# Roots and halves through PSUM, heads in pairs, DMA transposes of q and k, and values one pair back

## What is computed

```python
x = _rmsnorm(tokens, norm_w)
q = x @ Wq
k, v = jnp.split(x @ Wkv, 2, axis=-1)          # 16 heads of 64
q = _head_rmsnorm(q, q_gamma); k = _head_rmsnorm(k, k_gamma)
sim = jnp.einsum('bhid,bhjd->bhij', q, k)
sim = jnp.tanh(sim / SOFTCLAMP) * SOFTCLAMP
attn = jax.nn.softmax(sim * DIM_HEAD ** (-0.5), axis=-1)
out = jnp.einsum('bhij,bhjd->bhid', attn, v)
return out.transpose(0, 2, 1, 3).reshape(b, n, HEADS * DIM_HEAD) @ Wo
```

## Time and profile before

| | before |
|---|---|
| median of 3 runs | 1263.25 us (1262.8 to 1263.63) |
| the profiled execution | 1261.8 us, its span 1259.8 us |
| busy, share of the span | PE 93%, ACT 86%, DVE 82%, POOL 73% |
| matmuls | 13897 |
| mean granted TensorE clock | 0.992 of full |

### The profile page before, as it was taken

The page is one execution under the profiler, slowest core; times in us unless marked ns, Lnnn a source line. Parts: engine busy times, 40 slices in busy tenths (PEclk is TensorE's granted clock), DMA queues, the critical chain, the costliest instruction groups (busy, mean ns, idle before and its releaser), DMA issues.

```text
span 1259.8 us, 36165 instructions
## 1 busy us (share of the span) xinstructions
PE 1165.6 (93%) x13897; PEld 972.3 (77%) x13897; DVE 1032.2 (82%) x2153; ACT 1082.2 (86%) x2055; POOL 917.6 (73%) x1105
## 2 busy tenths in 40 slices
PE   3789999999999999999999999999999999999988
PEld 2468887778877778878778878778878778878777
DVE  6788889888889888889888889888889888888862
ACT  3589898889898889888888988888988888988885
POOL 4477777777777777877777877777777777777663
PEclk9899999999999999999999999999999999999999
DMA  4000000000000000000000000000000000000000
GB/s 132 10 11 11 14 16 7 15 15 11 15 15 7 15 15 11 15 15 7 15 15 11 14 16 7 15 15 11 14 15 7 15 15 15 10 11 11 11 6 9
DMA packets 32224, 19.41 MB, mean 15 GB/s; under 512 B 3508, under 2 KB 31288, under 8 KB 32056
## 3 DMA queue, kind: packets, MB, share of 16 engines
q1 hardware_dynamic: 32056, 17.12, 4.7%
HBM read 12.13 MB, written 4.19 MB: 13 GB/s over the span
## 4 chain that ended last, share of the span: by engine, by line
PE 42%; DVE 25%; ACT 19%; issue 11%; POOL 1%; ACTq 0%; POOLq 0%
PE ps_scores L481 8%; ACT probs L563 6%; PE ps_aux L455 5%; DVE qk L729 4%; PE ps_aux L448 4%; PE ps_aux L406 4%; PE ps_y L525 4%; DVE heads_T L738 3%; DVE sel_rows L760 3%; DVE qk L694 3%; PE ps_aux L408 3%; PE ps_aux L407 3%; ACT L596 3%; DVE norm L667 3%; ACT hid L596 3%
## 5 line engine op out<-in xcount | busy, mean ns | idle before, releaser
L905 POOL TENSOR_TENSOR probs_lo<-probs 128x512 f16<-128x512 f32 x512 | 586.3, 1150 | 235.1 <-ACT probs L563 232.9
L555 ACT ACTIVATE clamped<-ps_scores 128x512 f32<-128x512 f32 x512 | 310.3, 606 | 124.5 <-PE ps_scores L481 124.4
L563 ACT ACTIVATE probs<-clamped 128x512 f32<-128x512 f32 x512 | 324.9, 635 | 0.4
L503 PE MATMUL ps_o<-v_hi,probs 128*128 128x65 bf16 x2048 | 240.0, 195 | 4.5 <-DVE o_sb L706 2.7
L504 PE MATMUL ps_o<-v_lo,probs 128*128 128x64 bf16 x2048 | 239.2, 193 | 0.0
L505 PE MATMUL ps_o<-v_hi,probs_lo 128*128 128x65 bf16 x2048 | 238.9, 194 | 0.0
L481 PE MATMUL ps_scores<-heads_T 64*128 64x256 f16 x3072 | 212.9, 271 | 14.2 <-ACT clamped L555 14.0
L406 PE MATMUL ps_aux<-w_hi,xhT_hi 128*128 128x512 f32 x384 | 191.5, 499 | 31.9 <-DVE qk L729 21.6
L503 PEld LDWEIGHTS ps_o<-v_hi,probs 128*128 128x128 bf16 x2048 | 192.1, 99 | 30.1 <-issue 18.2
L504 PEld LDWEIGHTS ps_o<-v_lo,probs 128*128 128x128 bf16 x2048 | 189.8, 99 | 5.0
L505 PEld LDWEIGHTS ps_o<-v_hi,probs_lo 128*128 128x128 f16 x2048 | 190.2, 98 | 0.0
(11 more groups left out here) (83 smaller groups left out, 2211.2 us busy)
## 6 DMA issues: line engine op xcount, KB each, us to landing
x_in<-in_L_attn_tokens_dram SPq DMA_DIRECT2D x32, 128.0 KB, 2.3
x_res<-in_L_attn_tokens_dram SPq DMA_DIRECT2D x32, 128.0 KB, 2.3
out_dram<-y_sb SPq DMA_DIRECT2D x32, 128.0 KB, 1.9
sel_raw<-xn SPq DMA_DIRECT2D x192, 4.0 KB
qk<-in_L_attn_Wkv_dram SPq DMA_DIRECT2D x2, 512.0 KB, 5.4
qk<-in_L_attn_Wq_dram SPq DMA_DIRECT2D x1, 512.0 KB, 3.6
qk<-in_L_ffn_W_dram SPq DMA_DIRECT2D x2, 256.0 KB
hid<-in_L_attn_q_gamma_dram SPq DMA_DIRECT2D x1, 512.0 KB, 7.0
```

Of the source, the lines that this page charges most:

```text
L503: pe.matmul(full, hi[:, col], v_hi[:, par, u, h], start=(u == 0), stop=False)
L555: nc.scalar.activation(clamped[:, buf], ps_scores[:, s % SCORE_BANKS], ACT.Tanh).then_inc(clamp_done, 1)
L563: nc.scalar.activation(probs[:, buf], clamped[:, buf], ACT.Exp, bias=LIFT, scale=SOFTCLAMP * DH ** -0.5).then_inc(probs_done, 1)
L905: g.tensor_tensor(probs_lo[:, buf], probs[:, buf], probs[:, buf].bitcast(BF16)[:, 1::2], ALU.subtract).then_inc(lo_made, 1)
```

## The change

Heads go in twos: a step has 8 slots, each with a pair. Tanh and exp take both banks of scores as one instruction of 1024 columns, `clamped` has one buffer and `probs` two pairs. The values of a pair come one slot later, at the end of the slot, and are divided in the slot after. `ps_o` is one bank in place of two. In the rest of that bank lie `rnorm`, `minus_half_norm2` and `newton_a`; the bank freed is `ps_n`. The roots start from the PSUM tile in two seeds and take nine instructions on VectorE; GpSimd no longer has a part in them. `normalise` does one pair at a time, from `qk` into `ps_n`, four pairs ahead of the scores; ScalarE rounds `ps_n` to f16 (`half`), VectorE subtracts (`halves`), and SyncE turns each half with a DMA transpose into `heads_T` (`turn_heads`); the matmul transposes `qkT` are gone. The selection and the normalisation of the input go from VectorE to GpSimd, and the turned inputs `xhT` and `xnT` share one task `xT`. Since TensorE must not write a bank that VectorE uses, `values` waits for the steps of its slot that touch `ps_o`.

```diff
+RING = 2
+VALUES_LAG = 1
+DIVIDE_LAG = 2
+
+SCALAR_STEPS = [
...
+    [("tanh",), ("half",), ("exp",), ("hid", 0, 0), ("hid", 1, 0)],
...
 VECTOR_STEPS = [
...
+    [("halves",), ("divide",), ("newton", 0), ("newton", 1), ("newton", 2), ("newton", 3), ("newton", 4),
+     ("newton", 5), ("normalise",)],
...
 POOL_STEPS = [
...
+    [("bias",), ("lo",)],
+    [("select",), ("lo",)],
...
-        ps_o = ctx.enter_context(nc.psum_tensor("ps_o", [P, 2, 512], F32))
+        ps_o = ctx.enter_context(nc.psum_tensor("ps_o", [P, 512], F32))
         ps_aux = ctx.enter_context(nc.psum_tensor("ps_aux", [P, AUX_BANKS, 512], F32))
+        ps_n = ctx.enter_context(nc.psum_tensor("ps_n", [P, 512], F32))
...
-                elif kind == "qkT":
-
-                    if k % 2 == 0:
-                        wait(pe, qk_normed, 4 * b + k // 2 + 1)
-                    for j in range(2):
-                        for t in range(TT):
-                            at = j * HEADS * DH + k * P
-                            ins = pe.transpose(bank[:, (j * TT + t) * P:(j * TT + t + 1) * P],
-                                               qk[:, par, t, at:at + P], ident[:])
...
             def scores(st, pair):
...
-                wait(pe, qkT_split, PAIRS * b + pair + 1)
-                wait(pe, clamp_done, HEADS * b + 2 * pair)
+                wait(pe, heads_turned[pair % 4], 32 * ((PAIRS * b + pair) // 4 + 1))
+                wait(pe, clamp_done, PAIRS * b + pair)
...
-            def values(st, ahead, h):
+            def values(st, s, ahead, pair):
 
                 b, par, _ = st.batch(ahead)
-                pair = h // 2
-                if h == 0:
+                if pair == 0:
                     wait(pe, v_split, 4 * b + 4)
-                wait(pe, lo_made, HEADS * b + h + 1)
-                if h % 2 == 0:
-                    wait(pe, o_normed, PAIRS * b + pair - 1)
-                buf = h % RING
-                hi = probs[:, buf].bitcast(BF16)[:, 1::2]
-                for t in range(TT):
-                    at = (t * 2 + h % 2) * (DH + 1)
-                    full = ps_o[:, pair % 2, at:at + DH + 1]
-                    for u in range(TT):
-                        col = slice(u * seq + t * P, u * seq + (t + 1) * P)
-                        pe.matmul(full, hi[:, col], v_hi[:, par, u, h], start=(u == 0), stop=False)
-                        pe.matmul(full[:, 0:DH], hi[:, col], v_lo[:, par, u, h], start=False, stop=False)
-                        ins = pe.matmul(full, probs_lo[:, buf, col], v_hi[:, par, u, h],
-                                        start=False, stop=(u == TT - 1))
+                wait(pe, lo_made, PAIRS * b + pair + 1)
+                wait(pe, o_normed, PAIRS * b + pair)
+                n = st.batch(0)[0]
+                wait(pe, qk_normed, min(PAIRS * n + s + NORMALISE_LEAD + 1, PAIRS * batches))
+                if s == 2:
+                    wait(pe, seed_made, min(2 * (n + 2), 2 * batches))
+                if s in (3, 4):
+                    wait(pe, newton_step, min(9 * (n + 2) - (3 if s == 3 else 0), 9 * batches))
...
+            def turn_heads(st, ahead, pair):
+
+                b, _, _ = st.batch(ahead)
+                wait(sp, scores_done, 2 * PAIRS * (b - 1) + 2 * pair + 2)
+                for half, made in enumerate((half_hi_made, half_lo_made)):
+                    sp.wait_ge(made, PAIRS * b + pair + 1)
+                    sp.dma_start(heads_T[:, half, pair].rearrange("p t j n -> p (t j) n"),
+                                 halves16[:, pair % 4, half].rearrange("p a n -> p (a n)"),
+                                 transpose=True).then_inc(heads_turned[pair % 4], 16)
...
+            def tanh(st, pair):
+                b, _, _ = st.batch(0)
+                wait(act, scores_done, 2 * PAIRS * b + 2 * pair + 2)
+                wait(act, probs_done, PAIRS * b + pair)
...
+            def half(st, ahead, pair):
+                b, _, _ = st.batch(ahead)
+                act.wait_ge(qk_normed, PAIRS * b + pair + 1)
+                wait(act, heads_turned[pair % 4], 32 * ((PAIRS * b + pair) // 4))
+                nc.scalar.copy(halves16[:, pair % 4, 0].rearrange("p a n -> p (a n)"), ps_n[:]).then_inc(half_hi_made, 1)
...
+                wait(dve, newton_step, 9 * b + k)
+                if k % 3 == 0:
+                    v.tensor_tensor(newton_a, newton_r[:], minus_half_norm2, ALU.mult).then_inc(newton_step, 1)
+                elif k % 3 == 1:
+                    v.tensor_tensor(newton_a, newton_a, newton_r[:], ALU.mult).then_inc(newton_step, 1)
+                else:
+                    if k == 8:
+                        wait(dve, qk_normed, PAIRS * b)
+                    v.scalar_tensor_tensor(rnorm if k == 8 else newton_r[:], newton_a, 1.5, newton_r[:],
+                                           ALU.add, ALU.mult).then_inc(newton_step, 1)
+
+            def normalise(st, ahead, pair):
 
                 b, par, _ = st.batch(ahead)
-                if c == 0:
-                    dve.wait_ge(newton_step, 12 * b + 12)
+                if pair == 0:
+                    dve.wait_ge(newton_step, 9 * b + 9)
                     dve.wait_ge(q_scaled, 4 * b + 4)
                     dve.wait_ge(k_copied, 4 * b + 4)
-                part = qk[:, par].rearrange("p t (j n) -> p (t j) n", j=2)[:, :, c * 4 * DH:(c + 1) * 4 * DH]\
-                    .rearrange("p a (h d) -> p a h d", d=DH)
-                r = rnorm[:].rearrange("p (a h) -> p a h", h=HEADS)[:, :, 4 * c:4 * c + 4]
-                v.tensor_tensor(part, part, r.unsqueeze(3).to_broadcast([P, 2 * TT, 4, DH]), ALU.mult)\
-                    .then_inc(qk_normed, 1)
+                wait(dve, half_lo_made, PAIRS * b + pair)
+                r = rnorm.rearrange("p (a h) -> p a h", h=HEADS)[:, :, 2 * pair:2 * pair + 2]
+                v.tensor_tensor(ps_n[:].rearrange("p (a h d) -> p a h d", h=2, d=DH),
+                                pair_of_qk(par, pair).rearrange("p a (h d) -> p a h d", d=DH),
+                                r.unsqueeze(3).to_broadcast([P, 2 * TT, 2, DH]), ALU.mult).then_inc(qk_normed, 1)
+
+            def halves(st, ahead, pair):
+
+                b, _, _ = st.batch(ahead)
+                dve.wait_ge(half_hi_made, PAIRS * b + pair + 1)
+                v.tensor_tensor(halves16[:, pair % 4, 1].rearrange("p a n -> p (a n)"), ps_n[:],
+                                halves16[:, pair % 4, 0].rearrange("p a n -> p (a n)"), ALU.subtract)\
+                    .then_inc(half_lo_made, 1)
```

More of the change, by code:

```diff
@@ L70 @@
-STAGE = {2: "turn", 1: "front", 0: "attn", -1: "back"}
+PER_BATCH = {"xT": 1, "q": 4, "k": 4, "v": 4, "oT": 4, "low": 2, "hid": 2}
+STAGE = {3: "load", 2: "turn", 1: "front", 0: "attn", -1: "back"}
 SCORE_BANKS = 2
-RING = 4
-VALUES_LAG = 3
-VECTOR_STEPS = [
[L80 to L95, removed]
+RING = 2
@@ L423, in aux @@
                 done = aux_filled[kind]
-                if kind in ("xhT", "xnT"):
+                if kind == "xT":
                     wait(pe, xn_made, b + 1)
                     for t in range(TT):
-                        ins = pe.transpose(bank[:, t * P:(t + 1) * P], xh[:, t] if kind == "xhT" else xn[:, par, t],
-                                           ident[:])
+                        pe.transpose(bank[:, t * P:(t + 1) * P], xh[:, t], ident[:])
+                    for t in range(TT):
+                        ins = pe.transpose(bank[:, seq + t * P:seq + (t + 1) * P], xn[:, par, t], ident[:])
                 elif kind in ("q", "k"):
@@ new lines, in values @@
+                for j in range(2):
+                    h = 2 * pair + j
+                    hi = probs[:, buf, j].bitcast(BF16)[:, 1::2]
+                    for t in range(TT):
+                        at = (t * 2 + j) * (DH + 1)
+                        full = ps_o[:, at:at + DH + 1]
+                        for u in range(TT):
+                            col = slice(u * seq + t * P, u * seq + (t + 1) * P)
+                            pe.matmul(full, hi[:, col], v_hi[:, par, u, h], start=(u == 0), stop=False)
+                            pe.matmul(full[:, 0:DH], hi[:, col], v_lo[:, par, u, h], start=False, stop=False)
+                            ins = pe.matmul(full, probs_lo[:, buf, j, col], v_hi[:, par, u, h],
+                                            start=False, stop=(u == TT - 1))
@@ new lines, in run @@
+            def run(st):
+                for s in range(PAIRS):
+                    for what, *k in SCALAR_STEPS[s]:
+                        if what == "tanh":
+                            if "attn" in st.stages:
+                                tanh(st, s)
+                        elif what == "exp":
+                            if "attn" in st.stages:
+                                exp(st, s)
+                        elif what == "half":
+                            normed = ahead_of(st, s, NORMALISE_LEAD - 1)
+                            if normed:
+                                half(st, *normed)
```

(6 more changed lines are left out.)

470 lines of the change are left out of this document (226 added, 244 removed), and 13 rows, old and new, of the table AUX.

## The result

The changed kernel takes 1671.87 us (median of 4 runs, 1671.69 to 1675.47) against 1263.03 before on the same chip (1260.56 to 1263.63): 1.3249 times as long, 95% interval 1.3224 to 1.3274. Forecast was 1709, range 1570 to 1910. The profiled execution took 1671.78, with a span of 1669.8 us and a mean granted clock of 0.93.

What follows compares the result with a forecast made beforehand. The prediction took a ring of waits through four engines as the bound: 32 batches of 49.2 us, 54 for start and end, 76 for TensorE's low clock, span 1705, with a profile-to-median correction 1709 us; range 1570 to 1910.

Steps and rivals of the forecast that it cites:

- What bounds it: In the changed kernel a circle of waits through four engines, not busy time, bounds the batch at 49.2 us.
- The turn of the ring: Circle scores, tanh, half, halves, divide, normalise, values, next scores: 5.38 us in slots 5 and 7, eight slots 49.2.
- The clock: TensorE's pauses before the values bring the half clock: 1.19 us a slot, two slots a batch, 76 us in all.
- All three slots named: Slots 1 to 3, where TensorE was to pause 2.9, 3.1 and 3.7 us before the values.
- the rule that the prediction cites: On TensorE, idle gaps between bursts of matmuls bring the half clock back, so every burst starts cold.
- GpSimd is no part of it: GpSimd's low parts, 2.3 us, begin when exp ends and are wanted only at the end of the next slot.
- The transposes: 16 DMA transposes a batch on SP's queue, 2.3 us each, 37 us, hidden under the batch of 49.2.
- The rival with 2102 us: DMA transposes at 4 us each bound the kernel, 64 us a batch; chance 0.17.
- the clock that stays down: TensorE's clock stays low through all slots, 305 us on top, 1937 us; chance 0.12.
- The one that stays up: TensorE's clock stays up, leaving the circle of waits alone, 1632 us; chance 0.18.
- Start and end: Time of the span outside the 32 batches, 54 us, taken over from the kernel before.
- The rival "faster": VectorE's normalise runs a slot ahead, so TensorE less its transposes bounds: 1108 us; chance 0.04.

Runs made afterwards that it cites:

- run 2: ScalarE's half put ahead of tanh in every slot, against the changed kernel: 1396.3 us, ratio 1.107 to the kernel before.
- run 4: Changed kernel with the three root tiles in SBUF and without the values' waits for normalise, seeds and Newton steps: 1369.5 us, ratio 1.084 to before.
- run 5: Changed kernel with the next slot's scores issued ahead of this slot's values on TensorE, roots still in PSUM: 1215.8 us, ratio 0.962 to before.
- run 8: Changed kernel with every DMA transpose done a second time into a spare tile: 1679.3 us, ratio 1.328 to before.
- run 12: Changed kernel with scores ahead of values, divide ahead of halves, half behind tanh in slots 0 and 1, slot 1's halves and normalise earlier: 1172.4 us.
- run 3: Changed kernel with the three root tiles moved from PSUM to SBUF, the values' waits kept: 1997.2 us, ratio 1.583 to before.

## Why the prediction was right, step by step

- **What bounds it.** Right. No engine is the bound. The chain of waits after has 35% "issue" and no engine over 21%, and breaking the circle at one place (runs 2, 4, 5) took 275 to 456 us off, though in run 2 it opened in six slots of eight only.
- **The turn of the ring.** Right to 0.2 us a batch: 49.2 forecast, 49.02 measured at the full clock. That it is so near is luck in part, since the errors go both ways: slot 2 took 6.26 us where 6.57 was forecast, the others are off by 0.15 at most (the terms written for slot 6 add up to 5.5, not 5.6; it took 5.72). In slot 2 the two seeds and the w_eff update add 0.92 us from divide to normalise where 1.19 was charged, as each begins before the one ahead of it has ended. In slots 2 to 4 the first value matmul begins 0.26 us after normalise, in slots 0, 1, 5 and 7 the 0.15 of the forecast. Tanh was 1.025 for 1.05 us, exp 1.067 for 1.08, half 0.586 for 0.59, halves 0.689 for 0.68. Normalise, bounded by 0.65 and 0.68, took 0.689; it lies with the rows that have a PSUM operand. That the 1309 ns of the old normalise, with both inputs in SBUF, might hold waits for GpSimd was not thought of. The trace of before shows that they do: the 35 of its 128 that began with GpSimd idle took 1.22 us, the others 1.34 on average and up to 2.03. The bound of 0.65 should have been 0.61; the forecast took the other one.
- **The clock.** The step was right in kind and half again too large: 76 us charged, about 49 measured. The 28 batches from 149.88 to 1565.49 last 50.56 us on average against the 49.02 at the full clock, 1.54 x 32 = 49. Two falls a batch were charged, and there were 49 in the 28 batches, 1.75 each; but a fall cost 0.88 us and not 1.19. Why it cost less shows in slot 2 at 824.07 of after (granted clock of three parts of the slot, TensorE alone):

```profile
824.07:826.60 2.53, 2.53 (x21) 0.59 0.26 52
826.60:828.50 1.90, 1.90 (x13) 0.65 0.28 55
828.50:830.66 2.16, 1.03 (x28) 1.00 0.45 96
```

  Its scores took 1.09 in place of 0.83 us, but the transposes and products behind them lay in TensorE's free time, and when the values came the clock was up again: 6.52 us, no more than forecast at the full clock. The prediction charged scores and both heads' values at the low level, 1.19 us a fall; in this slot only 0.26 reached the ring. All three slots named had pauses, of 2.48, 2.48 and 2.56 us in the batch at 608.61 where 2.9, 3.1 and 3.7 were estimated. Not every such pause brings a fall: that batch stayed at 1.00. The falls moved about, and most batches stand at 0.93 or 0.97. By the rule that the prediction cites every batch would pay; this one did not.
- **GpSimd is no part of it.** Right, though the profile seems to contradict it: the values wait 75.2 us, and their weight loads 218.6, "for probs_lo". In slot 2 above, the wait that ended at 829.78 is put down to the low parts that ended at 829.65. They are those of this slot's own pair; the values take the pair before, whose low parts were ready at 822.10. Normalise ended at 829.52, and the values follow it by 0.26, as they do in slots 2 to 4 of the other batches. It was taken for GpSimd because that came last. The 17% for GpSimd in the chain of waits have this same step in them at 827.76. It holds for all of the 28 batches: in slots 0 to 5 and 7 the first value matmul begins 0.15 or 0.26 us after normalise (0.42 at most), and the low parts that it needs had been ready for 3.8 us or more.
- **The transposes.** Right: 2.5 us each for 2.3, hidden, and run 8 shows how far. The estimate of 0.5 us from a bandwidth is not the time of one transfer. The rival with 2102 us is out, and so is the clock that stays down (1937). The one that stays up (1632) is out by the falls in the trace and not by the time: the measured 1671.87 lies 40 us above it and 37 under the forecast.
- **Start and end.** 54 us forecast; 1669.8 - 32 x 50.6 = 50.6.
- **The rival "faster"** named the right condition: from a turn below 4.71 us a slot TensorE is the bound. Its price, 1108 us, took 32.94 us a batch, 31.18 of work and as much idle time as before; run 12 measured 31.93 of work in 34.70. The transposes' busy time of 4.74 us a batch was worth 4.0 of TensorE's 35.92.
- **Not seen:** that the cheapest way out is the order of two steps on TensorE (run 5), and that the PSUM bank keeps VectorE clear of GpSimd.

## What to carry to other kernels

When a change adds a wait, write down what is queued behind it on the waiting engine and follow that through the others; if it comes back to the releaser, sum one turn of the circle and compare it with the busiest engine's work. To mend such a ring, look first for the work that others need and move it ahead of the wait (here the next scores, 456 us); removing the wait (run 4) gave 302, since the place of the roots had a price of its own. Then ask whether a second step closes the same ring, as in slots 0 and 1 of run 2. An order that helps while a ring is closed may cost once it is open, so measure it again after every move.

## What had not been expected of the hardware

- A VectorE instruction on two SBUF inputs that starts during a GpSimd one waits out the rest of it: 0.23 us became 1.82, normalise 0.69 became 1.38 on average. With one input in PSUM its length varied by 14 ns over a whole run (683 to 697 ns, 256 of them, 222 of which began during a GpSimd instruction).
- A tensor_scalar of 64 columns from SBUF to SBUF, with one tensor input, was held too: L687 took 1.74 us mean in run 3, and 0.22 in after with its output in PSUM, though all 32 began during a GpSimd instruction in both runs. For this form the place of the output does count.
- DMA transposes of 128 KB land after 2.5 us in the median and overlap: 32 in 50.9 us.
